# A two-layer attention and mixture-of-experts kernel: router logits one step later, tails zeroed per half, expert results in block order, picks and sums spread over batches

## The reference

```python
x = x + tanh(g_xattn[0]) * L0_xattn(layernorm(x), ctx, ctx)   # 16 heads, rotary, band of +-32, softmax
x = x + tanh(g_ffn[0])   * L0_ffn(layernorm(x))               # 64 experts of width 88, top 8 of 4 of 8 groups
x = x + tanh(g_xattn[1]) * L1_xattn(layernorm(x), ctx, ctx)   # 16 heads, full softmax over 64 keys
x = x + tanh(g_ffn[1])   * L1_ffn(layernorm(x))               # 8 experts of width 512, top 2
```

## Time and profile before

| | us |
|---|---|
| runs: median (lowest to highest) | 1736.67 (1734.85 to 1751.07) |
| the profiled execution | 1753.41 |
| its span, first to last instruction | 1751.6 |
| PE busy | 1496.1 (85%) |
| DVE busy | 1030.6 (59%) |
| ACT busy | 855.2 (49%) |
| POOL busy | 830.8 (47%) |

### The profile page before, as it was taken

One profiled execution on the slowest core, in us unless ns is written; L12 is line 12 of the kernel. 1 busy time (PEld: TensorE's weight loads), 2 busy tenths in 40 slices (PEclk: granted clock), 3 DMA queues, 4 the chain that ended last, 5 costly groups with the idle time before them and its releaser, 6 DMA issues. The chain is left out here.

```text
span 1751.6 us, 31609 instructions
## 1 busy us (share of the span) xinstructions
PE 1496.1 (85%) x9341; PEld 1081.1 (62%) x9341; DVE 1030.6 (59%) x2853; ACT 855.2 (49%) x1887; POOL 830.8 (47%) x910
## 2 busy tenths in 40 slices
PE   5888888598778976766688888879999999999998
PEld 3666665387768876755466656645565565555655
DVE  4567667564457656566346565335666676656646
ACT  3545444132222322221455556446776777757756
POOL 1155546777712178654765652023444444434432
PEclk9988888599899998887777877656999999979969
DMA  6335511256655565553322210000000000000000
GB/s 178 76 103 154 161 45 37 65 151 190 197 161 148 156 170 150 148 143 97 110 77 70 57 45 22 1 0 1 7 1 7 1 6 6 1 6 6 0 7 7
DMA packets 215597, 129.97 MB, mean 74 GB/s; under 512 B 55490, under 2 KB 201986, under 8 KB 215442
## 3 DMA queue, kind: packets, MB, share of 16 engines
q1 hardware_dynamic: 139122, 60.88, 12.7%
q10 hardware_dynamic: 59904, 33.58, 6.6%
q0 software_dynamic: 16416, 33.65, 6.4%
HBM read 67.19 MB, written 60.82 MB: 73 GB/s over the span
## 5 line engine op out<-in xcount | busy, mean ns | idle before, releaser
L1501 POOL TENSOR_TENSOR wring<-weights,wring 128x256 fp32r<-128x256 f32 x256 | 240.2, 939 | 342.4 <-ACT wring L976 342.3
L1471 POOL DMA_INDIRECT expert_rows<-xn2T,slot x256 | 247.9, 968 | 89.0 <-issue 81.7
L1425 DVE TENSOR_TENSOR hsplit<-work,hsplit 128x512 fp32r<-128x512 f32 x256 | 177.4, 693 | 141.2 <-ACT hsplit L983 140.7
L983 ACT ACTIVATE hsplit<-work 128x512 fp32r<-128x512 f32 x256 | 161.1, 629 | 162.5 <-PE bank L724 158.9
L1444 DVE TENSOR_TENSOR work<-work,bank 128x512 f32<-128x512 f32 x256 | 175.9, 687 | 75.0 <-ACT work L1005 47.9
L936 ACT ACTIVATE arena<-bank 128x176 f32<-128x176 f32 x224 | 65.4, 316 | 299.5 <-PE bank L673 246.6
L1005 ACT ACTIVATE work<-bank,b 128x512 f32<-128x512 f32 x256 | 172.0, 672 | 14.5 <-PE bank L724 13.9
L695 PE MATMUL bank<-wexp,arena 88*128 x768 | 115.2, 297 | 70.4 <-DVE arena L1344 70.1
L1484 POOL DMA_INDIRECT xn2T<-expert_rows,slot x128 | 127.6, 997 | 70.8 <-issue 37.5
L831 ACT ACTIVATE work<-bank 128x512 f32<-128x512 f32 x128 | 76.3, 596 | 160.9 <-PE bank L497 160.5
L695 PEld LDWEIGHTS bank<-wexp,arena 88*128 88x128 f32 x768 | 102.0, 207 | 79.4 <-issue 79.0
(11 more groups left out here) (190 smaller groups left out, 3164.3 us busy)
## 6 DMA issues: line engine op xcount, KB each, us to landing
arena<-expert_rows SPq DMA_DIRECT2D x384, 64.0 KB
expert_rows<-arena ACTq DMA_DIRECT2D x384, 64.0 KB
expert_rows<-zero SPq DMA_DIRECT2D x256, 64.0 KB
arena<-in_ctxT ACTq DMA_DIRECT2D x32, 256.0 KB, 2.6
expert_rows<-xn2T,slot POOLq DMA_INDIRECT x256
weights<-in_mix SPq DMA_DIRECT2D x8, 512.0 KB
wexp<-in_mix SPq DMA_DIRECT2D x15, 176.0 KB
x<-in_x SPq DMA_DIRECT2D x4, 512.0 KB, 7.9
```

Of the source, the lines that this page charges most:

```text
L983: act.activation(hsplit[:, c % 2, 0, :], work2[:, c % 2, :], ACT.Copy).then_inc(S["h_hi"], 1)
L1425: dve.tensor_tensor(hsplit[:, c % 2, 1, :], work2[:, c % 2, :], hsplit[:, c % 2, 0, :].bitcast(F32), ALU.subtract).then_inc(S["h_lo"], 1)
L1471: pool.indirect_dma_start(xs, bass.IndirectOffsetOnAxis(ap=slot[:, t, k:k + 1], axis=0), xn2all[:, t, :].bitcast(I32), None).then_inc(s_sc ...
L1501: pool.tensor_tensor(wsplits[:, place, 1, 0:CW[1]], weights[:, c * CW[1]:(c + 1) * CW[1]], wsplits[:, place, 0, 0:CW[1]].bitcast(F32), ALU ...
```

## The change

The change has six parts.

1. In both attentions the transpose of the normed rows, the logits and their copies belong to group R = j-4 in place of B = j-3: a step later. They use bank `w3`. On PE `turn(0)` now opens a step, then come `back_turn`, `scores`, `back_logits`, and only then `project_v`. `norm2_apply` stays in step B. On ACT the copies move to the head of the step.
2. In layer 0 `rank_rows` moves to group K, between `project_q` and `values(3)`, and DVE's `key_rows`, `top_rows` and `slot_rows` move from the head to the end of the step. POOL starts scattering a step later.
3. The tails of a half are zeroed when its counts are known: the first half's in step 12 of attention 0, the second half's after step 20, all 64 of them ahead of the first `load_rows`. The loads of layer 1's small weights move behind `load_rows(24)`.
4. Results go to a new DRAM tensor `expert_results` in block order, by one DMA a batch in place of four. ACT, not DVE, copies them out of PSUM (`keep_rows`). The gather's row numbers are moved to the new order by `shift_keys`, 4 parts a half on DVE, and `block_tables` makes `shift_row` for that.
5. POOL's `pick_weights` of tiles 0 to 15 stand between the scatters that are left after attention 0, one after each 8, and those of tiles 16 to 31 follow at once, ahead of the gathers. DVE's `sum_picks` of tiles 0 to 15 stand in batches 4, 6, ... 34 and those of tiles 16 to 31 in batches 36 to 51.
6. `combine` works on one tile (8 operations, each waiting for the one before), from batch 56 on at every third batch, and in 13 steps of attention 1 in place of 8. Only one late step is left in the mixture.

```diff
-LATE = (GROUPS + 3, GROUPS + 4)
+LATE = GROUPS + 4
-PICK_AT = 26
-COMBINE_AT = HRTB + 9
+PICK_AT = 4
+SHIFT_AT = HRTB + 4
+COMBINE_AT = HRTB + 8
...
@@ SP @@
-            sp.wait_ge(s_tab, 1)
-            for e in range(0, E0, 4):
-                zero_tails(e, 4)
-            sp.wait_ge(s_slot, GROUPS)
-            small(1, layers[1])
+            for h in range(HALVES):
+                sp.wait_ge(s_tab, h + 1)
+                for e in range(0, E0, 4):
+                    zero_tails(h * E0 + e, 4)
...
-                if XR <= m < XR + E0 // 2:
-                    zero_tails(E0 + (m - XR) * 2, 2)
+                if m == HRTB // 2:
+                    sp.wait_ge(s_slot, GROUPS * 2)
+                    small(1, layers[1])
...
@@ PE, attention @@
+                    if v: turn(0)
+                    if r: back_turn()
+                    if m: scores()
+                    if r: back_logits()
                     if f: project_v()
-                    if v: turn(0)
-                    if m: scores()
                     if v: values(0); turn(1)
...
                     if f: project_q()
+                    if k and L: back_weights()
+                    if k and L == 0: rank_rows()
                     if v: values(3)
                     if m: shift(3)
-                    if b: back_turn()
-                    if b: back_logits()
-                    if k and L: back_weights()
-                    if r and L == 0: rank_rows()
...
@@ ACT, attention @@
+                    if v: copy_turned(0)
+                    if r: copy_xn2()
+                    if f: norm_apply()
+                    if r: read_logits()
                     if f: mask_values()
-                    if v: copy_turned(0)
-                    if f: norm_apply()
                     if v: copy_turned(1)
...
                     if b: norm2_apply()
+                    if k and L: keep_weights()
                     if m: exps(3)
-                    if b: copy_xn2()
-                    if b: read_logits()
...
@@ ACT, experts @@
+                def keep_rows(m):
+                    act.wait_ge(b_y, SHB + m + 1)
+                    if m >= YR:
+                        act.wait_ge(s_store[m % YR], m // YR * 16)
+                    act.activation(yb[:, m % YR, :, :].rearrange("p b d -> p (b d)"), bank[7][:, :], ACT.Copy).then_inc(b_yc, 1)
...
-                    for b in range(NB):
-                        act.dma_start(flat[bass.ds(rows[b], P * D)].rearrange("(p d) -> p d", d=D), yb[:, m % YR, b, :].bitcast(I32)).then_inc(s_store[m % YR], 16)
+                    act.dma_start(ys[m * NB * P:(m + 1) * NB * P, :].rearrange("(b p) d -> p b d", p=P), yb[:, m % YR, :, :].bitcast(I32)).then_inc(s_store[m % YR], 16)
...
@@ DVE, experts @@
-                    else:
-                        keep_rows(m)
-                    if 0 <= m - PICK_AT < HTILES:
-                        sum_picks(m - PICK_AT)
+                    if 2 <= n < 6:
+                        shift_keys(0, n - 2)
+                    if SHIFT_AT <= m < SHIFT_AT + 4:
+                        shift_keys(1, m - SHIFT_AT)
+                    if 0 <= m - PICK_AT < 2 * HTILES and (m - PICK_AT) % 2 == 0:
+                        sum_picks((m - PICK_AT) // 2)
+                    if 0 <= m - PICK_AT - 2 * HTILES < HTILES:
+                        sum_picks(m - PICK_AT - HTILES)
...
-                    if m >= COMBINE_AT and (m - COMBINE_AT) % 6 == 0:
-                        pick_and_combine((m - COMBINE_AT) // 6)
+                    if m >= COMBINE_AT and (m - COMBINE_AT) % 3 == 0:
+                        combine((m - COMBINE_AT) // 3)
...
@@ POOL @@
-            scatter_some(TILES * TOPK0, GROUPS)
-            for t in range(HTILES):
+            picked = 0
+            while sent < TILES * TOPK0:
+                sent = scatter_some(TOPK0, GROUPS)
+                if picked < HTILES:
+                    pick_weights(picked)
+                    picked += 1
+            for t in range(picked, TILES):
                 pick_weights(t)
```

More of the change, by code:

```diff
@@ L324, in slots, with late @@
                 step(j, *has_group(j))
[L326 to L328 removed]
+        def late(step):
+            step(LATE, *has_group(LATE))
         def pairs(eng, group):
```

284 lines of the change are left out of this document (158 added, 126 removed).

## The result

The changed kernel took 1691.45 us (median of four runs, 1675.24 to 1706.49), the kernel before 1743.87 (1734.85 to 1758.37) in runs beside it. By these medians it is faster by 52 us, a ratio of 0.970, where 98 us were forecast. The changed kernel's runs fall in two pairs, 1675.24 and 1676.60 us at a granted clock of 0.86 and 1706.31 and 1706.49 at 0.85; with the faster pair alone the ratio is 0.960, with a 95% interval of 0.947 to 0.973, and the gain some 69 us. The profiled execution, 1676.60 us, has a span of 1674.8 us, 76.8 less than that of before and some 25 more than the medians give, since it lies at the low end of its runs, and that of before above the median of its own.

A forecast was written before the change was run, and what follows sets the result against it. Attention and experts were taken as bound by waits between engines, the mixture by PE. Attention 0's 39, attention 1's 34 and the experts' 26 less 1 make 98 us off 1736.7: 1639 us, range 1600 to 1690.

The forecast's parts named there:

- Attention 0: First attention stage: 15 full steps each save 2.6 us, 1.4 of waits and 1.2 of clock; 39 us, from 21 to 57.
- The clock: Attention 0: running at half speed costs 2.4 us a step; between 0 and 2.4 comes back, 1.2 taken.
- The waits: Attention 0: PE's waits before the transpose and logits shrink, and project_v no longer follows read_logits; 1.4 us a step saved.
- The start of the experts: Ahead of the first routed batch: shift_keys and the tables make batch 0 come 3 us later.
- The picks: Experts, batches 0 to 34: POOL waits some 48 us before pick 2, then DVE waits for picks; 16 us lost.
- After the picks: Experts, batches 34 to 95: 234 us against 275.7, in three windows of 54, 21 and 129 plus 30 for sums.
- The period: Experts, time per batch after the picks: 3.3 to 3.4 us, set by ACT's copy and a store landing in 2.6.
- The gathers: POOL, end of the experts: start near batch 50, take 165 us, to 783, ahead of batch 95 at 798.
- slow-store rival: Experts: one 256 KB store takes 4.67 us from issue to landing, a batch 5.4; 1755 us in all; chance 0.06.
- Attention 1: Second attention stage: with sums by tile a step falls from 18.4 to 15.8 us over 13 steps; 34 us, from 15 to 45.
- attention gives only its waits back: Rival for both attention stages: the clock stays as it is; 61 us gained in all, 1676 us; chance 0.21.
- The mixture: Last stage: PE busy 582 of 592 us, only one small late step touched; it stays as it is.

## Why the prediction was right and wrong

The side was right. The time is at the edge of the range: the ratio of 0.960 on the 1736.67 us that the forecast started from gives 1668, within 1600 to 1690, while the median of all four runs, 1691.45, is 1.5 above it. The gain was 52 to 69 us where 98 were forecast. That it came this near is in part luck. In the profiled pair attention 1 missed by 68.5 us, the experts gave 22.2 more than forecast, and the mixture, forecast at nothing, gave 27.5. In the order of its steps:

- **Attention 0: right in the total, with the terms off.** 37.8 for 39. A step saves 3.34 us and not 2.6. The clock gave back all of its 2.4 (PE's busy time fell by 2.43), not the half that I took: it is 1.00 in these eleven steps. The waits gave 0.91 and not 1.4. The eleven steps make 36.7 and those behind them 6.0; against that the first four took 55.9 us where they took 51.1. So fewer steps gained than the 15 counted, and each gained more. The experiment adds, for three steps, that the transpose alone moved back costs 0.2 a step, and transpose and logits 1.4.
- **The start of the experts: right.** Batch 0 comes 56.5 us behind the first transpose of the stage, before 53.5; 3 were forecast.
- **The picks: right.** A wait of 50.6 (48 forecast), a pick per 11.5 (11.4), batches 0 to 34 163.1 us against 147.7: 15.4 lost, and 18.4 with the 3 of the later start, where 16 were forecast for both.
- **After the picks: the mechanism right, two terms too large, and one limit missed.** Batches 34 to 50 took 54.6 (54) and 50 to 56 19.0 (21). From 56 to 95 it was 134.5 and not 159. The period was to be 3.3, from a landing of 2.6; the rows above give 1.9 to 2.4, so the store's loop stayed below PE's 3.05. The Trainium skill, "DMA: Bandwidth & Descriptors", section "Anatomy of one DMA", has a fit for GpSimd's DMAs that gives an estimate of 2.6 for this size; the times measured here, for a DMA that ACT issues, are shorter, and they decide. And a sum was to cost 2.3 a tile on the path; (134.5 - 39 x 3.05) / 13 is 1.2. The rest lay in DVE's free time, which I had allowed 0.3 for. The gathers, "not the limit" by the forecast, ended 4.4 us behind the start of batch 95's copy and ended the stage. The slow-store rival read the DMA engines' share of the earlier trace rows as 0.53 to 0.61; the second of its rows has 0.48.
- **Attention 1: wrong, in sign.** The step that failed is "Were the stall all there is, a step would fall to the 14.8 us of the quiet one", and the 15.8 made from it; measured were 21.3 us a step, against 18.4 before. I took one quiet step at full clock for the state that the stage would be in once the sum's stall was gone. The runs showed that the stall is not the lever: with seven eighths of every sum left out the stage took as long. What went with the loss is the clock, which fell from 0.75 to 0.59 while PE's idle time fell too, by 5.6 us. I had no rival in which attention 1 gets slower; the nearest, that attention gives only its waits back, still had it at -15.
- **The mixture: nearly the same work**, 27.5 us shorter by the clock alone. The forecast's remark that the profiled execution of before lies above the median was there; that an execution of after may lie below its own was not weighed.

What stays open is why the clock in attention 1 is lower in the changed kernel than before, 0.59 against 0.75 and 0.68 in two pairs. The place of the logits may be part of it, by one comparison that is barely above its noise. That `project_v` comes later, the order on ACT, or sums by tile in place of pairs were not tried alone. All experiments ran where other stalls reach into every stage, so none of them tests the first pair of profiles itself.

## What to carry to other kernels

A single step that ran at full clock is no forecast for a stage: in two stages with nearly the same step program the clock was 1.00 in the one and 0.59 in the other. Sum a stage twice, at each of the two clocks that its rows show, and give both as outcomes, with a sign each. And before a stall is priced at its full length, ask which wait takes its place; here PE's idle time stayed at 48 to 54 us through four edits that each eased what looked like its cause, and was 44 with two of them together.

## What the runs showed of the hardware

A low clock can last while PE is busy all the time. In the changed kernel, in attention 1 and at the start of the mixture:

```profile
1026.00:1060.00 34.00, 32.66 (x212) 23.83 (x210) 15.80 (x60) 17.34 (x41) 2.78 (x6) 0.50 0.01 1
1112.00:1150.00 38.00, 38.00 (x79) 21.23 (x79) 15.00 (x22) 17.71 (x34) 10.75 (x12) 0.54 0.00 1
```

In the second row PE is busy 38.00 of 38 us by the records, and at a mean of 0.54 it is granted 1.2 GHz for nearly all of it. The Trainium skill, "TensorE: Matmul & The Clock Gate", section "What's actually happening", says that activity releases the throttle; in these rows it was not released by work that the records show as without a gap, so PE's busy time in a profile does not tell which of the two levels it runs at. The granted clock has to be read beside it.

The other finding is the stalls: in these later runs the same two kernels took 2128 to 2137 and 2000 us in place of 1744 and 1691, with ACT, DVE and PE idle for 2 to 8 us at a time while POOL issued indirect DMAs, and a batch at 5.9 to 7.0 us in place of 3.05. That an order of work which lets POOL's DMAs pause now and then is the better one there was not shown in the time of a run, only in the shared batches. But an order that is tuned where the stalls don't occur should be timed again where they do.
